# The call order of five engine queues laid out anew in an attention and mixture-of-experts kernel

## The reference

```python
xn = _layernorm(x, axis=-1)
x = x + attention(xn, Wq, Wk, Wv, Wo) + ffn(xn, router, experts, shared expert)
# attention: 32 query heads, 8 key/value heads, head size 128, rotary turn of q and k,
attn = softmax(where(causal, q @ k.T / sqrt(128), -inf)); out = (attn @ v) @ Wo.T
# ffn: softmax router + bias, the best 2 of 4 groups, the best 2 of 16 experts for each token,
h = silu(xt @ w1 + b1) * (xt @ w2 + b2); y = y + gate * (h @ w3 + b3)
# and one shared expert of inner size 256 for all tokens
```

## Time and profile before

| what | value |
|---|---|
| time, median of 3 runs | 890.32 us (890.21 to 890.57) |
| time of the profiled execution | 890.17 us |
| its span, first to last instruction | 888.4 us |
| mean granted TensorE clock, of full | 0.996 |
| busy: PE, DVE, POOL, ACT | 874.4, 680.8, 526.9, 431.0 us |
| first matmul of head 0, of head 1, of head 7 | 70.88, 159.76, 794.33 us |
| first matmul of the last product | 884.42 us |

### The profile page before, as it was taken

How to read it: one execution, slowest core, us unless ns; L and a number is a source line. 1 busy time by engine, 2 the same in 40 slices (tenths; PEclk the granted TensorE clock), 3 DMA queues, 4 the chain that set the end, 5 groups by cost and what they waited for, 6 DMA issues and landing times.

```text
span 888.4 us, 17519 instructions
## 1 busy us (share of the span) xinstructions
PE 874.4 (98%) x5086; PEld 748.5 (84%) x5086; DVE 680.8 (77%) x1615; ACT 431.0 (49%) x1082; POOL 526.9 (59%) x638
## 2 busy tenths in 40 slices
PE   8998999999999999999999999999999999999998
PEld 7787888888889888888888888888888888888876
DVE  6698877687677877779777786768777787677986
ACT  3504544554535645554554545455453564445443
POOL 5914786475654765548554675456565476553662
PEclk9998999999999999999999999999999999999999
DMA  9910223143223522335222353234322352230242
GB/s 332 327 48 1 83 106 137 44 152 104 90 77 109 169 87 86 85 97 175 85 91 79 114 164 89 77 83 132 122 89 77 96 170 94 82 93 22 95 146 93
DMA packets 52161, 97.73 MB, mean 110 GB/s; under 512 B 5920, under 2 KB 17824, under 8 KB 52128
## 3 DMA queue, kind: packets, MB, share of 16 engines
q1 hardware_dynamic: 49568, 88.94, 31.7%
q0 software_dynamic: 2560, 8.39, 2.9%
HBM read 74.76 MB, written 22.54 MB: 110 GB/s over the span
## 4 chain that ended last, share of the span: by engine, by line
PE 90%; DVE 7%; issue 1%; ACT 1%; DMA 0%; SPq 0%; DVEq 0%; ACTq 0%
PE bank L1998 10%; PE bank L2000 10%; PE bank L1999 10%; PE bank L2225 7%; PE bank L2132 7%; PE bank L2229 6%; PE bank L2134 6%; PE bank L2226 6%; PE bank L2133 6%; PE bank L2193 5%; PE bank L2206 4%; PE bank L2209 4%; PE bank L2207 4%; PE bank L2179 2%; PE bank L2256 1%
## 5 line engine op out<-in xcount | busy, mean ns | idle before, releaser
L645 POOL TENSOR_SCALAR prob<-prob,rsum 128x128 f32<-128x128 f32 (+3 forms) x256 | 143.6, 579 | 87.0 <-DVE rsum L1487 86.2
L885 ACT ACTIVATE prob<-bank,nmax 128x128 f32<-128x128 f32 (+3 forms) x256 | 134.0, 529 | 110.4 <-DVE nmax L1481 103.5
L1481 DVE CUSTOM_DVE_ANT_0 bank<-bank,causal 128x128 f32<-128x128 f32 (+3 forms) x256 | 122.9, 503 | 29.6 <-PE bank L2000 26.6
L1509 DVE TENSOR_TENSOR pT_lo<-bank,pT_hi 128x512 fp32r<-128x512 f32 x160 | 109.5, 685 | 27.5 <-ACT pT_hi L905 27.0
L905 ACT ACTIVATE pT_hi<-bank 128x512 fp32r<-128x512 f32 x160 | 95.4, 597 | 71.2 <-PE bank L2193 53.8
L2132 PE MATMUL bank<-xT_hi,wq_lo 128*128 128x512 f32 x256 | 104.2, 407 | 2.0 <-DVE kT_lo L1472 1.7
L2225 PE MATMUL bank<-wo_lo,oT_hi 128*128 128x512 f32 x256 | 105.5, 412 | 0.6 <-ACT oT_hi L896 0.6
L628 POOL TENSOR_TENSOR w_lo<-w_raw,w_hi 128x1024 fp32r<-128x1024 f32 x31 | 74.6, 2407 | 52.3 <-ACT w_hi L940 52.3
L2134 PE MATMUL bank<-xT_hi,wq_hi 128*128 128x512 f32 x256 | 101.1, 395 | 0.0
L2229 PE MATMUL bank<-wo_hi,oT_lo 128*128 128x512 f32 x256 | 101.1, 395 | 0.0
L2133 PE MATMUL bank<-xT_lo,wq_hi 128*128 128x512 f32 x256 | 100.5, 393 | 0.0
(11 more groups left out here) (219 smaller groups left out, 2323.4 us busy)
## 6 DMA issues: line engine op xcount, KB each, us to landing
w_raw<-w SPq DMA_DIRECT2D x31, 512.0 KB, 3.4
wq_raw<-wq SPq DMA_DIRECT2D x32, 256.0 KB, 4.0
wo_raw<-wo SPq DMA_DIRECT2D x32, 256.0 KB, 2.7
xg<-x_slots SPq DMA_DIRECT2D x31, 256.0 KB, 3.6
w_raw<-w SPq DMA_DIRECT2D x31, 256.0 KB, 2.7
eb<-b SPq DMA_DIRECT2D x31, 256.0 KB, 3.9
y_slots<-eb SPq DMA_DIRECT2D x31, 256.0 KB, 2.6
x_slots<-pairs SPq DMA_DIRECT2D x3, 2048.0 KB, 16.0
```

The source lines that it names most:

```text
L645: last = nc.gpsimd.tensor_scalar(row, row, rsum[:, stat(b, i, h)], 1.0, ALU.mult, ALU.mult)
L885: last = nc.scalar.activation(prob[n % 2][:, h, 0:P * (i + 1)], bank[S_BANKS[use % 2]][:, 256 * k:256 * k + P * (i + 1)], ACT.Exp, bias=nm ...
```

## The change

Only the order of the calls in the 15 lists is another one; the multiset of operations on every engine is the same. The calls that do nothing (`collect` outside head 7, `place_x` outside head 0, `combine_two` outside head 7, the expert calls of tiles that do not exist) are left out. The diff in its core:

```diff
@@ -693,106 +634,92 @@
                         gather(n, 1)
 
             def first_head(g):
-                collect(g, 3)
+                place_x(g, 0)
                 normalise(g, 0, 0)
+                normalise(g, 0, 1)
                 add_k(g, 1, 0)
                 add_q(g, 1, 0)
-                normalise(g, 0, 1)
-                place_x(g, 0)
+                add_k(g, 1, 1)
                 normalise(g, 0, 2)
-                add_k(g, 1, 1)
                 add_q(g, 1, 1)
+                split_kv(g + 1)
+                add_q(g, 1, 2)
+                split_q(g + 1, 0)
                 normalise(g, 0, 3)
-                add_q(g, 1, 2)
-                split_kv(g + 1)
...
                 normalise(g, 1, 2)
                 add_k(g + 1, 0, 1)
-                collect(g, 1)
-                collect(g, 2)
+                place_x(g, 2)
                 add_q(g + 1, 0, 1)
-                split_q(g + 1, 3)
                 add_q(g + 1, 0, 2)
                 normalise(g, 1, 3)
...
+            def last_head(g):
+                lo_w12(tile_of(g, 0))
+                normalise(g, 0, 0)
+                normalise(g, 0, 1)
+                add_q(g, 1, 0)
+                add_k(g, 1, 0)
                 add_k(g, 1, 1)
+                lo_w3(tile_of(g, 0))
                 normalise(g, 0, 2)
                 add_q(g, 1, 1)
-                split_kv(g + 1)
...
-                split_q(g + 1, 1)
-                split_q(g + 1, 2)
-                lo_w12(tile_of(g, 3))
-                add_q(g + 1, 0, 0)
                 collect(g, 0)
...
-                add_q(g + 1, 0, 1)
-                split_q(g + 1, 3)
-                add_q(g + 1, 0, 2)
-                lo_w3(tile_of(g, 4))
-                normalise(g, 1, 3)
-                add_q(g + 1, 0, 3)
-                collect(g, 1)
-
-            def last_head(g):
-                lo_w12(tile_of(g, 0))
-                place_x(g, 1)
-                add_k(g, 1, 0)
-                normalise(g, 0, 0)
-                lo_w3(tile_of(g, 0))
-                add_q(g, 1, 0)
-                normalise(g, 0, 1)
-                add_k(g, 1, 1)
-                normalise(g, 0, 2)
-                add_q(g, 1, 1)
-                normalise(g, 0, 3)
-                place_x(g, 2)
-                add_q(g, 1, 2)
-                collect(g, 0)
-                add_q(g, 1, 3)
                 collect(g, 1)
                 normalise(g, 1, 3)
                 collect(g, 2)
                 normalise(g, 1, 2)
+                normalise(g, 1, 1)
                 collect(g, 3)
-                normalise(g, 1, 1)
...
                 first_places(g, 2)
-                maxima(g, 1, 2, 3)
                 turn_k(g + 1, 0, 1)
+                maxima(g, 1, 3, 0)
+                maxima(g, 1, 3, 1)
                 inverse_sums(g, 1, 2)
-                maxima(g, 1, 3, 0)
+                lo_oT(g, 1, 0)
...
                 turn_q2(g + 1, 0, 1)
+                maxima(g, 1, 3, 3)
                 lo_pT(g, 1, 2, 0)
-                combine_two(g, 1)
+                lo_pT(g, 1, 2, 1)
                 lo_kT(g + 1, 0)
-                lo_oT(g, 1, 1)
-                maxima(g, 1, 3, 3)
...
-                add_b12(tile_of(g, 1))
-                expert_product(tile_of(g, 1))
                 expert_hidden(tile_of(g, 1))
+                add_out(g - 1, 1, 3)
                 maxima(g, 0, 3, 2)
+                lo_kT(g, 1)
+                lo_hT(tile_of(g, 1))
+                lo_q(g, 1, 1)
+                lo_pT(g, 0, 2, 0)
+                maxima(g, 0, 3, 3)
+                add_b3(tile_of(g, 1))
+                lo_oT(g, 0, 1)
                 lo_wo(g, 2)
-                lo_kT(g, 1)
-                lo_q(g, 1, 1)
-                maxima(g, 0, 3, 3)
-                lo_pT(g, 0, 2, 0)
-                lo_hT(tile_of(g, 1))
                 lo_wo(g, 3)
...
+                values(g, 0, 1, 0)
+                transpose_k(g, 1)
+                transpose_p(g, 0, 2, 0)
+                transpose_p(g, 0, 2, 1)
+                transpose_h(tile_of(g, 1))
+                values(g, 0, 1, 1)
+                project_out(g, 0, 0, 0)
...
-                scores(g, 0, 3, 3)
-                transpose_k(g, 1)
-                transpose_p(g, 0, 2, 0)
-                transpose_p(g, 0, 2, 1)
-                expert_down(tile_of(g, 0))
-                values(g, 0, 1, 1)
```

1226 lines of the change are left out of this document (564 added, 662 removed).

## The result

The changed kernel takes 903.71 us (901.67 to 904.45, 4 runs), the kernel before 890.45 us (890.21 to 891.68, 4 runs): ratio 1.0142 (95% interval 1.0123 to 1.0162). It is 1.4% slower, where 888.1 us was forecast.

The account below looks back on a forecast made before the run. TensorE was taken as the bound, busy 874.4 of 888.4 us. On the profiled scale, 890.17 − 5.1 (loop) + 0.8 (first head) + 2.1 (last head) = 888.0, hence forecast 888.1 us, range 884.9 to 891.0.

Parts of the forecast that it names:

- Net 0.85 a pass, 5.1 us for six: Loop: gains of 1.0 us a pass less 0.15 of waits, 5.1 us saved over six passes (3.0 to 6.5).
- I count the whole 0.55 and the 0.15 as gone: Loop: late query projection (0.55 us, behind a weight split before kT_lo) and transpose_h (0.15) vanish, 0.7 us a pass.
- For every product on TensorE I set the matmul time ... against the chain between: Loop: slack check found two project_kv places closest, about 0.1 us to spare; loss taken as 0.15 us a pass.
- the turns wait in the loop: Rival, chance 0.17: both project_kv places lose 0.3 us, 0.6 a pass instead of 0.15, giving 890.8 us.
- the slower rival: Rival, chance 0.08: each project_kv place loses 0.55 us, 1.1 a pass instead of 0.15, giving 893.8 us.
- Fourteen runs of transposes fewer ... give 0.3 us: Loop: merging runs of transposes saves 0.02 us per run, 0.3 us a pass (0.14 to 0.5).
- First head: First head: scatters ahead of normalisation, gate reductions moved and a late add_q, net +0.8 us (−0.3 to +1.6).
- The gates' stall: First head: three gate reductions ahead of maxima delay scores by 0.69 us; moved behind them, gain 0.7 us.
- Last head: Last head: 5.8 us of new waits from GpSimd's queue against vanishing old stalls, taken as +2.1 us (−0.5 to +3.5).
- Against it the old stalls of this head go: Last head: TensorE's old standstill beyond issue and transpose runs, 3.3 us, is credited against 5.8 us of new waits.
- a rival with 0.08: Rival, chance 0.08: the last head's new 2.7 us wait drops TensorE's clock to half, costing 2.1 us, giving 890.2 us.
- The ends lose nothing: Rival, chance 0.15: first head even, last head even or 0.5 us better, giving 885.2 us.

Follow-up runs that it names:

- e1: Kernel before with the new call lists of all five engines in the loop body alone; 0.31% slower than the kernel before.
- h1: e1 with load_w3 of the second tile swapped ahead of load_b3 on SyncE; 0.12% faster than the kernel before.
- g4: Kernel before with lo_kT(g,1) moved ahead of lo_wo(g,2) on VectorE in the loop; 0.15% faster than the kernel before.
- f7: e1 with load_w3 of the second tile moved on SyncE far ahead, before load_wq(g,0) and the store; 0.88% slower than the kernel before.
- h2: h1 with lo_pT(g,0,3,1) moved ahead of expert_product and add_out on VectorE; 888.62 us, 0.27% faster than the kernel before.
- e2: Kernel before with the new call lists of all five engines in the first head alone; 0.33% slower than the kernel before.
- h3: e2 with the scatters place_x(0,0) moved on GpSimd behind add_k(0,1,1); 0.31% slower than the kernel before.
- e3: Kernel before with the new call lists of all five engines in the last head alone; 0.71% slower than the kernel before.
- g2: e2 with place_x(0,0) on GpSimd back behind the normalisation of blocks 0 and 1; 0.97% slower than the kernel before.
- g3: Kernel before with the new list of GpSimd alone in the last head, other engines' lists old; 1.04% slower than the kernel before.

## Why the prediction was wrong

The time lies above the range and on the other side. By its own steps:

- **"Net 0.85 a pass, 5.1 us for six"** is the step that failed: −5.1 against +2.8 measured (e1), half of the error. Its gain was taken as certain and its loss was looked for at the wrong places. *"I count the whole 0.55 and the 0.15 as gone"*: the split on VectorE was taken from the front of kT_lo, but kT_hi on ScalarE was put behind a weight copy, and that behind a transfer whose place in SyncE's queue I had not read; h1 shows that this transfer's place is worth 0.4%. Even in the old lists the stall gives 1.3 us and not 3.3 when it is removed (g4). The 1.25 us of the split in the earlier trace rows was no price of the split either: from 407.96 to 409.26 GpSimd was at a split of its own, the overlap is 0.70 us, and 0.55 more make 1.25. Behind lo_kT, in g4, the same split takes 0.68 us. The prediction priced VectorE's operations without asking what GpSimd does at that moment; such an overlap is behind the waits of f7 and a part of the bank wait.
- *"For every product on TensorE I set the matmul time ... against the chain between"*: that chain was made of the operations that a product depends on, each starting at once. The two closest places by it, project_kv with 0.1 us to spare, never waited in the nine profiles with the new lists in the loop. With the old lists, which left 2.77 and 4.01 us for a chain of 2.3, it waits in seven of ten profiles, up to 0.79 us. The query projection waited although it had 0.4 us to spare by it (2.15 less 1.75), and the bank of the second transpose does not appear in the prediction at all. At both places the operation stood behind others in its own engine's queue (expert_product and add_out ahead of lo_pT, hi_w3 ahead of hi_kT). The rival "the turns wait in the loop" and the slower rival had the right direction at the wrong place, and both were too small: they add 0.45 and 0.95 us a pass to the forecast, where 1.3 were needed (7.9 us for six).
- *"Fourteen runs of transposes fewer ... give 0.3 us"*: without the starts that come 0.15 us and more late a pass has 105.07 us before and 105.04 in h2, means of six. So the merging gave about 0.1 us or less, and it brought the bank wait of 0.41.
- **First head**: +0.8 forecast, +2.9 measured (e2). Right in place, the scatters ahead of the first normalisation, but for 0.5 us I followed block 0 alone; the normalisation of block 1, behind it in the same queue, waited as well, 3.1 us in both (2.1 and 1.0 of lost starts). These waits are not all of it, since h3 has neither and loses as much; what the first head loses beyond them stays open. The gates' stall went as said. The 0.7 to 1.0 us of the late add_q were 0.2.
- **Last head**: +2.1 forecast, +6.3 measured (e3). The waits I had priced came nearly as priced: block 3 2.5 us (2.7), the end 1.6 (1.45), scores 0.53 (0.45); block 2 0.46 (1.0). What failed is the sentence *"Against it the old stalls of this head go"*: the 3.3 us of credit did not come, since values waits for lo_pT behind combine_two as before and longer (1.37 us at one place, 0.86 before). The rest is the clock: a rival with 0.08, right in kind, in all four profiles that have the whole new last head, at 1.0 to 2.8 us by the starts of the 512-column matmuls that came 0.2 us late.
- "The ends lose nothing" was refuted by e2 and e3.
- The sums of issue do not come out of the prices that stand beside them: with the counts of the trace, 291, 24, 180 and 129 matmuls of 512, 384, 256 and 128 columns in a pass, they give 103.8 us and not 104.4, and 81.3 and 86.1 in the two ends, not 82.05 and 86.85. The forecast uses them only in the credit of 3.3 us in the last head, which failed for the reason above.

## What to carry to other kernels

When an order of calls is laid out anew, follow for each wait the queue of the engine that makes the operand, one engine at a time and as far as the queue that starts the transfers: the slack between producer and consumer on the busiest engine says little if the producer stands third in line. A call that waits for a transfer's landing holds all that is behind it, so put loads that do not need it ahead of it (two calls exchanged gave 0.4% here), but not ahead of what it waits for (the same load put ahead of the store cost 0.57%). A duration read in a trace is not the operation's own price where VectorE and GpSimd run splits at the same time: 0.68 us became 1.25 to 2.8. And lists that were laid out together are best changed at single places and by measurement: of nine single moves here one gave, by the medians, what its theory said or more.

## What the runs showed that I had not expected

A wait of TensorE of 5.7 to 5.8 us was followed by a stretch at 0.43 us for 512 columns (g2, g3). So were two waits of 1.33 and 0.90 us close together in the changed kernel. But in e3 the same two waits (1.26 and 0.90) were not: there TensorE keeps its pace of 0.23 us behind them, and the clock falls 26 us later, behind a wait of 1.43 us near the end, which in the changed kernel (1.36 us) is followed by no fall. So which wait a fall follows differs from one execution to the next, and the longest wait does not decide it; in the last head it cost 1.0 to 2.8 us, in g2 2.4. The Trainium skill, page "TensorE: Matmul & The Clock Gate", Part 1, says that the idle array goes back to the half rate; g2 and g3 agree, 0.43 us where the earlier trace rows has 0.23.

VectorE's split of a weight takes 0.68 us, also beside GpSimd's normalisation of the probabilities, which reads one tile (0.68). When a GpSimd operation that reads two tiles began before it, it takes until that one ends and 0.55 us more, in all 12 cases in the loop of the kernel before and all 18 of e1, f7 and h2, up to 2.8 us (f7).

With a load of 256 KB issued 1.2 us ahead of a store, the step behind the store's landing could go 3.8 to 4.6 us after the store in the six passes of f7, and 2.9 to 3.4 us in e1. So an "early" transfer is not free on a queue whose next call waits for a landing.
